# Attention output computed with tokens on partitions and added to x from its PSUM bank

## The reference

```python
x = x + 0.5 * ffn(layernorm(x))      # layer 0 of the kernel's expert code
x = x + attention(layernorm(x))      # Q = x@Wq+bq, 16 heads of 128, K and V of 4 groups; softmax(Q K^T / sqrt(128)) V, then @ Wo + bo
x = x + 0.5 * ffn(layernorm(x))      # layer 1
# ffn: 64 experts; the 8 largest router logits of each token choose its experts and weights;
# an expert takes its first 32 tokens (in the order of tokens), h = silu(x w1) * (x v1), y = h w2;
# the weighted y are added back to their tokens
```

## Time and profile before

| | |
|---|---|
| median of 3 runs | 665.5 us (663.27, 665.5, 667.88) |
| the profiled execution | 667.9 us, span 666.0 us |
| busy of the span | PE 94%, PE weight load 79%, VectorE 75%, ScalarE 59%, GpSimd 8% |
| the chain that ended last | PE 72%, VectorE 12%, ScalarE 6%, DMA 6%, issue 2% |
| granted PE clock, mean | 0.971 |

### The profile page before, as it was taken

One profiled execution on the slowest core, in us unless ns is written; L12 is line 12 of the kernel. 1 busy time (PEld: TensorE's weight loads), 2 busy tenths in 40 slices (PEclk: granted clock), 3 DMA queues, 4 the chain that ended last, 5 costly groups with the idle time before them and its releaser, 6 DMA issues.

```text
span 666.0 us, 11671 instructions
## 1 busy us (share of the span) xinstructions
PE 626.7 (94%) x4320; PEld 525.8 (79%) x4320; DVE 498.3 (75%) x1309; ACT 391.1 (59%) x1053; POOL 52.4 (8%) x75
## 2 busy tenths in 40 slices
PE   8589999999999999999999999999999999887995
PEld 6367677999888888888888888888888888665774
DVE  6746668889988677887777788876778877773663
ACT  5634475767666566566556666666666656662441
POOL 3443000000000000000000000000000000134210
PEclk9689999999999999999999999999999999969998
DMA  8999940000000000000000000000000034266991
GB/s 318 341 416 419 376 153 1 2 1 1 0 1 1 1 1 0 1 1 1 0 1 1 1 0 1 1 1 0 1 1 2 0 127 190 110 207 228 419 376 48
DMA packets 27619, 62.50 MB, mean 94 GB/s; under 512 B 7014, under 2 KB 17382, under 8 KB 27558
## 3 DMA queue, kind: packets, MB, share of 16 engines
q1 hardware_dynamic: 25398, 55.97, 22.2%
q0 software_dynamic: 1664, 5.30, 2.1%
q10 hardware_dynamic: 496, 0.43, 0.3%
HBM read 54.34 MB, written 7.34 MB: 93 GB/s over the span
## 4 chain that ended last, share of the span: by engine, by line
PE 72%; DVE 12%; ACT 6%; DMA 6%; issue 2%; POOL 1%; SPq 0%; POOLq 0%; DVEq 0%; ACTq 0%
PE bank L1406 18%; PE bank L1408 17%; PE bank L1407 17%; PE bank L1462 7%; PE bank L1217 3%; DMA slots<-token_table,slot_index 3%; DMA down_r<-down_in 3%; PE bank L1257 2%; ACT probs L728 2%; PE bank L1225 2%; PE bank L1267 2%; ACT probsT_hi L739 1%; DVE q_lo L1073 1%; ACT q_hi L711 1%; DVE probsT_lo L1129 1%
## 5 line engine op out<-in xcount | busy, mean ns | idle before, releaser
L728 ACT ACTIVATE probs<-bank,negmax 128x256 f32<-128x256 f32 x256 | 121.4, 494 | 1.8 <-DVE negmax L1087 1.6
L739 ACT CAST probsT_hi<-bank 128x512 fp32r<-128x512 f32 x128 | 68.8, 590 | 70.9 <-PE bank L1462 70.9
L711 ACT ACTIVATE o_hi<-bank,bv 128x512 fp32r<-128x512 f32 x64 | 44.1, 690 | 69.2 <-PE bank L1408 69.2
L1129 DVE TENSOR_TENSOR probsT_lo<-bank,probsT_hi 128x512 fp32r<-128x512 f32 x128 | 81.7, 679 | 0.4 <-ACT probsT_hi L739 0.4
L1087 DVE TENSOR_REDUCE negmax<-bank 128x2 f32<-128x512 f32 x128 | 81.7, 679 | 0.0
L1095 DVE TENSOR_SCALAR probs<-probs,rowinv 128x256 f32<-128x256 f32 x256 | 73.0, 348 | 2.3
L1073 DVE SCALAR_TENSOR_TENSOR o_lo<-bank,bv,o_hi 128x512 fp32r<-128x512 f32 x64 | 48.0, 749 | 34.5 <-ACT o_hi L711 34.5
L1408 PE MATMUL bank<-k_hi,q_lo 128*128 128x256 f32 x256 | 72.4, 283 | 0.0
L1407 PE MATMUL bank<-k_lo,q_hi 128*128 128x256 f32 x256 | 72.3, 283 | 0.0
L1406 PE MATMUL bank<-k_hi,q_hi 128*128 128x256 f32 x256 | 72.2, 282 | 0.0
L1073 DVE SCALAR_TENSOR_TENSOR q_lo<-bank,bq,q_hi 128x512 fp32r<-128x512 f32 x64 | 47.9, 748 | 32.2 <-ACT q_hi L711 31.9
(11 more groups left out here) (184 smaller groups left out, 1294.9 us busy)
## 6 DMA issues: line engine op xcount, KB each, us to landing
up_r<-up_in SPq DMA_DIRECT2D x16, 768.0 KB, 9.3
down_r<-down_in SPq DMA_DIRECT2D x14, 512.0 KB, 11.1
up_q<-up_in SPq DMA_DIRECT2D x8, 768.0 KB, 8.8
up_o<-up_in SPq DMA_DIRECT2D x6, 768.0 KB, 14.6
down_q<-down_in SPq DMA_DIRECT2D x8, 512.0 KB, 9.6
token_table<-xn SPq DMA_DIRECT2D x16, 256.0 KB, 2.4
down_o<-down_in SPq DMA_DIRECT2D x6, 512.0 KB, 16.3
x<-x_in SPq DMA_DIRECT2D x4, 512.0 KB, 5.5
```

Source lines behind the costliest of these rows:

```text
L711: nc.scalar.activation(dst, src, ACT.Identity, bias=bias).then_inc(work_high, 1)
L728: nc.scalar.activation(probs[:, n % 2, t, :], scores_ps[head][:, qt * S:qt * S + S], ACT.Exp, bias=negmax[:, n % 2, t:t + 1], accum_out=ro ...
L739: nc.scalar.copy(probsT[0][:, head].rearrange("p c s -> p (c s)"), probsT_ps[head][:]).then_inc(probsT_high, 1)
L1129: nc.vector.tensor_tensor(probsT[1][:, head].rearrange("p c s -> p (c s)"), probsT_ps[head][:], probsT[0][:, head].rearrange("p c s -> p ( ...
```

## The change

The operands of the output product are exchanged: `o` is stationary and `wo` moves (256 columns), so that `out_ps[bb]` holds 128 tokens on partitions, with the two tiles of a batch side by side. All products run one step late with 12 matmuls of 256 columns. `yT`, its copy, its transposes and the `work_ps` banks they used are gone; VectorE adds `out_ps[bb]` to x directly, batch 0 at step 15 and batch 1 at step 1 of the next block. The bias is added to x beforehand from `bo_row`, a row of `bo` on all partitions, which ScalarE and two PE matmuls of layer 0 make. At step 12 the product is split around the projections, and at step 16 it comes after the second projection. For the last block, the moments of tiles 0 to 11 move into steps 11 and 12. The low halves of some weights are made a little earlier. In layer 1 the wide `take_tokens` comes ahead of the codes, and `keep_busy(16)` behind the narrow part becomes 12. `wait_for_gathers` waits for four gathers where it waited for two, and in layer 0 SP waits until the last group's weights have landed before it issues the loads of wk, wq, wv and wo.

```diff
@@ -354,7 +334,8 @@
         first_fills = [("xT", 0, 0), ("xT", 1, 0), ("k", 0, 0), ("q", 0, 0), ("q", 1, 0), ("v", 0, 0),
                        ("q", 2, 0), ("q", 3, 0), ("v", 1, 0)]
         SCORES_AT = 6
-        SPREAD_AT = (5, 6, 7, 9)
+        SPREAD_AT = (5, 6, 7, 10)
+        BIAS_AT = ((13, 14), (4, 8))
...
             def wait_for_gathers(layer):
 
-                for n in range(2):
+                for n in range(IN_FLIGHT - 1):
...
             for g in range(4):
@@ -448,6 +429,7 @@
                 load(0, g)
             for g in range(AHEAD, GROUPS):
                 load_when_free(0, g)
+            sp.wait_ge(home(0, GROUPS - 1)[2], 16 * loads_before(0, GROUPS - 1))
...
                 copy_logits(3)
-                if layer == 1:
-                    act.wait_ge(y_ready, 2 * BLOCKS)
+                if layer == 0:
+                    act.wait_ge(small_loaded, 64)
+                    for kd in range(KD):
+                        nc.scalar.activation(bo_row[:, kd * P:kd * P + P], ident[:], ACT.Identity, scale=0.0,
+                                             bias=bo[:, kd:kd + 1]).then_inc(bo_spread, 1)
+                else:
+                    act.wait_ge(y_raw, 2 * BLOCKS)
                     make_code_ident()
                 act.wait_ge(moments_ready, layer + 1)
...
                 act.wait_ge(moments_ready, 2 * layer + 1)
                 normalise(first, TILES)
                 warm(ACT.Silu)
+                if layer == 0:
+                    act.wait_ge(bo_crossed, 1)
+                    nc.scalar.copy(bo_row[:], bank[5][:, D:2 * D]).then_inc(bo_ready, 1)
                 act.wait_ge(slotsT_raw, sT_seen.add())
                 nc.scalar.copy(slotsT[:, 0, :, :].rearrange("p k t -> p (k t)"), bank[0][:, 0:KD * P]).then_inc(slotsT_ready, 1)
...
                 jobs = fills(n, last)
-                if i > 0 and n in (2, 3):
-                    act.wait_ge(y_raw, y_seen.add())
-                    take_output(n - 2)
...
                 for job in jobs:
                     take_fill(*job)
-                if i > 0 and n in (2, 3):
-                    uses[0] += 1
-                take_high(o[0][:, home_of_o(n), :, :], bv[:, kv:kv + 1])
+                take_high(o[0][:, n % 2, :, :], bv[:, kv:kv + 1])
...
             copy_tokens(3)
-            act.wait_ge(y_raw, y_seen.add())
-            for d in range(KD):
-                take_output(d)
             expert_layer(1)
...
             late_moments = moment_steps(4, TILES)
-            in_fill = {1: 3, 2: 4, 3: 5, 4: 6, 6: 7, 7: 8, 8: 9}
+            in_fill = {1: [3], 2: [4], 3: [5], 4: [6, 7], 5: [8], 6: [9]}
...
-            def add_output(i, d):
-
-                dve.wait_ge(y_ready, y_seen.add())
-                xa = x[:, i * 4:i * 4 + 4, d * P:d * P + P]
-                nc.vector.tensor_tensor(xa, xa, work_ps[uses[0] % 2][:].rearrange("p (t c) -> p t c", t=4), ALU.add).then_inc(work_taken, 1)
-                uses[0] += 1
-                taken.add()
-
-            def last_output(i):
-
-                for pair in range(2):
-                    dve.wait_ge(y_ready, y_seen.add())
-                    xa = x[:, i * 4 + 2 * pair:i * 4 + 2 * pair + 2, :].rearrange("p t d -> p (t d)")
-                    last = nc.vector.tensor_tensor(xa, xa, work_ps[uses[0] % 2][:], ALU.add).then_inc(work_taken, 1)
-                    uses[0] += 1
-                    taken.add()
-                nc.vector.sem_inc(attention_done, 1)
-                dve.wait_ge(work_taken, taken.now())
-                nc.vector.memset(last_token[:, 0:1], 0.0)
-                for t in range(4):
-                    last = nc.vector.bn_stats(stats[:, i * 4 + t, :], x[:, i * 4 + t, :])
-                return last
+            def add_bias(i, bb):
+
+                xa = x[:, 4 * i + 2 * bb:4 * i + 2 * bb + 2, :]
+                nc.vector.tensor_tensor(xa, xa, bo_row[:].unsqueeze(1).to_broadcast([P, 2, D]), ALU.add).then_inc(bias_added, 1)
+
+            def add_output(i, bb):
+
+                dve.wait_ge(y_raw, y_seen.add())
+                dve.wait_ge(bias_added, 2 * i + bb + 1)
+                xa = x[:, 4 * i + 2 * bb:4 * i + 2 * bb + 2, :].rearrange("p t d -> p (t d)")
+                nc.vector.tensor_tensor(xa, xa, out_ps[bb][:], ALU.add).then_inc(out_added, 1)
+
+            def spread_of(i, t):
+
+                dve.wait_ge(out_added, 2 * i + t // 2 + 1)
+                return nc.vector.bn_stats(stats[:, 4 * i + t, :], x[:, 4 * i + t, :])
...
@@ -1141,14 +1113,21 @@
                     take_fill(*job)
                 if n == 9 and not last:
                     normalise_tokens(i + 1)
-                if added and n in (2, 3):
-                    add_output(i - 1, n - 2)
-                take_low(*[t[:, home_of_o(n), :, :] for t in o], bv[:, kv:kv + 1])
-                if added and n in SPREAD_AT:
-                    dve.wait_ge(work_taken, taken.now())
-                    a = 4 * (i - 1) + SPREAD_AT.index(n)
-                    nc.vector.bn_stats(stats[:, a, :], x[:, a, :])
-
+                if i is not None and n in BIAS_AT[i > 0]:
+                    add_bias(i, BIAS_AT[i > 0].index(n))
+                if i is not None and n == 15:
+                    add_output(i, 0)
+                if i is not None and i > 0 and n == 1:
+                    add_output(i - 1, 1)
+                take_low(*[t[:, n % 2, :, :] for t in o], bv[:, kv:kv + 1])
+                if i is not None and i > 0 and n in SPREAD_AT:
+                    spread_of(i - 1, SPREAD_AT.index(n))
+                if last and n in (11, 12):
+                    for moment in steps_of_last[6 * (n - 11):6 * (n - 11) + 6]:
+                        moment()
+
+            steps_of_last = moment_steps(0, TILES - 4)
+            dve.wait_ge(bo_ready, 1)
             dve.wait_ge(x_final, 4)
             normalise_tokens(0)
             for n, job in enumerate(first_fills):
@@ -1157,17 +1136,22 @@
                     maxima(0)
                 if n == SCORES_AT + 1:
                     normalise_probs(0)
-                if n in in_fill:
-                    split_low(in_fill[n])
+                for m in in_fill.get(n, []):
+                    split_low(m)
             step(0)
...
             for n in range(1, STEPS):
                 step(n, BLOCKS - 1, last=True)
-            masks(1, 0, moment_steps(0, TILES - 4))
             shifts(0, TILES - 4)
-            tie(last_output(BLOCKS - 1))
+            for t in range(2):
+                spread_of(BLOCKS - 1, t)
+            masks(1, 0)
+            add_output(BLOCKS - 1, 1)
+            nc.vector.sem_inc(attention_done, 1)
+            spread_of(BLOCKS - 1, 2)
+            tie(spread_of(BLOCKS - 1, 3))
             steps = moment_steps(TILES - 4, TILES)
             masks(1, 1, steps[:7])
             masks(1, 2, steps[7:])
...
                     pe.wait_ge(x_loaded[u // 2], 16)
                 elif u >= TILES // 2 - 2:
-                    pe.wait_ge(work_taken, issued.now(back=TILES // 2 - 1 - u))
+                    pe.wait_ge(out_added, 2 * (BLOCKS - 1) + u - (TILES // 2 - 2) + 1)
...
                 logits_of(layer, 3)
+                if layer == 1:
+                    take_tokens()
...
                 last.then_inc(codes_raw, 1)
-
-                take_tokens(layer)
-                if layer == 1:
-                    keep_busy(16)
+                if layer == 0:
+                    pe.wait_ge(bo_spread, KD)
+                    for kd in range(KD):
+                        last = mm(bank[5][:, D + kd * P:D + kd * P + P], bo_row[:, kd * P:kd * P + P], ident[:], start=True, stop=True)
+                    last.then_inc(bo_crossed, 1)
+
+                if layer == 0:
+                    take_tokens()
+                else:
+                    take_narrow_tokens()
+                    keep_busy(12)
                 pe.wait_ge(first_ready, keys_seen.add())
...
-            def output_product(n):
-
-
+            def output_product(n, i, halves=range(2)):
+
+
+                n %= STEPS
                 kv, bb, hp = place(n)
-                on_chip(("o", n % STEPS))
+                on_chip(("o", n))
                 split_by(O_SPLIT[kv])
-                for d in range(KD):
+                if i > 0 and n in (0, 2):
+                    pe.wait_ge(out_added, 2 * i - 1 + bb)
+                for qt in halves:
                     for head in range(2):
-                        last = three(out_ps[d][:, bb * S:bb * S + S], [a[:, G * kv + 2 * hp + head, d * P:d * P + P] for a in wo],
-                                     [a[:, home_of_o(n), head, :] for a in o], n % STEPS == 0 and head == 0,
-                                     n % STEPS == STEPS - 1 and head == 1, shared=True)
-                if n % STEPS == STEPS - 1:
+                        h = G * kv + 2 * hp + head
+                        last = three(out_ps[bb][:, qt * D:qt * D + D], [a[:, n % 2, head, qt * P:qt * P + P] for a in o],
```

(39 more changed lines are left out.)

72 lines of the change are left out of this document (20 added, 52 removed).

## The result

The changed kernel took 658.51 us (median of 8, 656.42 to 661.2) against 667.27 for the kernel before (median of 8). One of those eight, at 2100 us, counts in the median and not in the ratio. The ratio is 0.9886, 95% interval 0.9862 to 0.9909, about 7.6 us less; by the medians it is 8.8. Four more sets of runs, each on another chip, gave 0.9906, 0.9871, 0.9876 and 0.9837. I had forecast 14.7 us; the change brings a little over half of that.

The account below looks back on a forecast made before the run. The PE was taken as the bound, with 72% of the chain. Attention -5.1, all behind it -9.9 and layer 0 +0.3 make -14.7 us, from the 665.5 median 650.8, forecast as 651 us, range 644 to 659.

Parts of the forecast that it names:

- Gathers and loads of layer 1: Layer 1: fourth gather's 3.5 us wait goes, loads then end late; -9.9 us for all behind attention, bounds -7 and -11.5.
- Routing, the first gather: Layer 1 routing: keys start earlier, tokens and fillers delay less, the table's landing limits; first gather -6.7 us, bounds -6.0 and -6.9.
- the 2.1 us of the masks: Layer 1 routing: moments leave VectorE's work ahead of the second masks, so the keys start about 2.1 us earlier.
- the 4.6 us of tokens and fillers: Layer 1 routing: wide tokens move ahead of the codes, fillers drop to 24, so the slot keys come 4.6 us sooner.
- Attention: All attention steps: sum of gains from dropped transposes and waits against dearer products, -5.1 us.
- Steps 2 and 3: Attention, blocks 1 to 3: yT transposes and work-bank wait go, 1.07 us less per step, six times, -6.4 us.
- the products: Other attention steps with output products: twelve matmuls of 256 columns cost 0.09 us more, 38 times, +3.4 us.
- the waits: Attention steps 12 and 16: moved output products shrink PE waits, 0.35 us in seven places, -2.4 us, bounds 0 and -3.
- The last block: Attention's last block: steps 11 and 12 have one product less, VectorE gets moments; -1.0 us, bounds 0 and -2.7.
- rival (c): Attention blocks 1 to 3: output products wait for o_lo in every step, +22 us, time about 674; chance 0.05.
- Layer 0: Layer 0: last group's weights land sooner, attention's weight loads start later; +0.3 us, bounds -0.7 and +2.5.
- rival (b): Attention: waits of steps 2, 3, 12 and 16 come back elsewhere, attention +1 to +3, time 657 to 660; chance 0.12.

Follow-up runs that it names:

- sets 2 to 4: Three sets of follow-up runs, each on its own chip beside the kernel before; the unchanged changed kernel took 658.91, 657.0 and 659.06 us in them.
- wait_two: Changed kernel with layer 1's loads held behind two gathers instead of four: 659.67 us, ratio 0.9888 to the kernel before.
- wait_five: Changed kernel with layer 1's loads held behind all five gathers issued at once instead of four: 658.43 us, ratio 0.9859 to the kernel before.
- changed_fifth: Changed kernel run unchanged a fifth time, on another chip: 656.2 us, ratio 0.9837 to the kernel before.
- before_again: Kernel before, unchanged, run again beside the changed kernel's third run: 664.72 us in one execution.
- routing_alone: Kernel before plus only layer 1's routing part (wide tokens ahead of codes, twelve fillers, loads behind the fourth gather): 662.76 us against 666.08, ratio 0.993.
- early_exps: Changed kernel with layer 1's exponentials taken by ScalarE after eight normalised tiles instead of twelve: 655.2 us, one run.
- wide_late: Changed kernel with layer 1's wide tokens behind the codes again and sixteen fillers: 663.68 us, ratio 0.9959 to the kernel before.
- attention_alone: Changed kernel with wide tokens behind the codes, sixteen fillers, loads behind two gathers and no SyncE wait in layer 0: 661.22 us, ratio 0.9903.
- moments_in_four: Changed kernel with the last block's moments in portions of 4, 4 and 3 instead of 6 and 5: 656.22 us, one run.
- set 5: Fifth set of runs: the unchanged changed kernel, 656.2 us, and the same without layer 0's SyncE wait, 654.26 us.
- sets 1 and 5: Set 1 ran single-edit kernels without an unchanged changed kernel (kernel before 666.08 us); set 5 has its own line.

## Why the prediction was wrong

The direction held, and 658.5 lies in the range, but the effect was put at nearly twice its size. By the steps of the prediction:

**Gathers and loads of layer 1: this step failed.** Of the 9.9 us for all behind attention, 3.2 were for what comes after the first gather, and 1.4 were measured. I took the 3.51 us wait for the fourth gather and 1.3 us of slow steps behind it as won in full, as if nothing else held the PE in those steps. What the runs showed in its place is a late semaphore ahead of the second slot step. It came in every kernel of sets 2 to 4, the kernel before among them, and was 1.6 to 3.0 us late in four of the five profiles of the changed kernel; in three of these four the half clock followed. The fourth gather lands while the PE is held by it, so the wait that I removed isn't there to be won: wait_two and wait_five moved the time by nothing measurable. From the first gather to the end the changed kernel with the late semaphore takes 62.5 us in the mean, the kernel before 62.7. Where it doesn't come, the term holds as far as one profile of the kernel before can tell: 4.3 to 4.9 us in the first four slot steps for the 4.8 forecast, and 59.8 us to the end in changed_fifth for 64.0. I had read one execution, the slowest of three, as the kernel; a second one (before_again) shows the other case.

I had also set the wait against a rule of the Trainium skill ("DMA: Bandwidth & Descriptors", "Queues, rings and completion order": an engine alternates between the queue rows it has work for) and let the row win. By the DMA packets of the traces the first gathers land 2.5 to 3.5 us after their issue, and the fourth and fifth, in the kernels that wait for two and so have loads beside them, after 5.0 to 6.6 us. They are slowed, but they don't stand behind all the loads, which last about 39 us. So the trace agrees with the rule, and a gather slowed in this way still cost 3.51 us in the one profile where the PE was there first.

The loads I had nearly right: their last packet is through at 639.2 in the first profile of the changed kernel (forecast 640.6), though their first one comes 1.0 us after the issue and not 2. In the changed kernel the last group waits for them by 0.24 us at most. In routing_alone it waits 1.65 us, and the half clock follows from 647.5 to 650.9; of its 4.8 us from the gathers only 0.9 reached the end.

**Routing, the first gather: right in kind, 1.6 us too large.** 6.7 forecast, 5.1 measured in all five profiles. VectorE lost 2.1 us to GpSimd's multiply, for which the sum had no term. early_exps shows that with these back the table's stores hold the gather, 0.1 us of gain, and with the stores reordered 1.0. Of the two parts the 2.1 us of the masks came out (2.2 to 2.5 in wide_late, though attention_alone lost them again at the half clock), and the 4.6 us of tokens and fillers did not: 3.0 in routing_alone, 2.7 from wide_late to the changed kernel.

**Attention: -5.1 forecast, -4.1 measured.** Steps 2 and 3 gave 1.08 each, 6.5 in all, as forecast; the products cost 0.09 a step as the row said, not 0.015 as by the 2.5 ns of the Trainium skill ("TensorE: Matmul & The Clock Gate", "Wait — 56ns, not 53.3ns?"), in 28 places and not 38 (+2.6 for +3.4); block 0 +1.9 for +1.8. Of the waits only step 16 improved, 9.73 to 9.26, and step 12 got 0.13 to 0.19 worse, since half a product is too little cover for xT_lo: -0.9 for -2.4, though step 10 gave 0.7 that I hadn't counted. The last block gave +0.2 for -1.0: step 11 lost its 1.27, steps 12 and 13 took 1.47 back. moments_in_four shows that 0.6 of that is the moments; in the rest the PE waits for probsT_lo of VectorE, 1.19 and 0.94 us, with no projection to cover it. The splits at the start gave 0.8 for 0.5, and rival (c), products that wait for o_lo, never showed. (Its time should have been 673, not 674.)

**Layer 0: +0.3 forecast, +1.5 measured.** The landing of wo (94.6, forecast 93 to 94) was seen, the rest of the queue not: wk, wq and wv are late for ScalarE too. Of the 1.5 us about 0.6 is the wait: from the first xn transpose to step 0 it is 16.4 us without it and 17.0 or more with it. By the medians of set 5 the kernel without the wait is 1.9 us faster; the two profiles of that set don't show where that comes from. Why step 0 is some 1 us later than before even then stays open; the starts scatter by over 1 us between executions of one kernel (106.8 and 105.3 before).

**The measure.** The forecast started from an execution of 667.9 us and was subtracted from the median. Part of what it removed was what made that execution slow. That 658.5 falls where rival (b) put it says nothing for (b): attention got 4.1 us shorter, not longer.

## What to carry to other kernels

Take a second profile before a wait is priced: a wait that differs between two executions of the same kernel can be won only in the executions that have it, and one that lies beside another wait is worth only what it sticks out. When several chains meet, an edit of one is worth only the distance to the next: here 1.6 us of VectorE's chain brought 0.1 us until the table's stores were moved too. And a wait set ahead of a queue delays everything behind it: list all that the queue carries, not only the transfer it is meant for.

## What the runs showed of the hardware

**Late semaphores.** In 13 of the 20 profiles the semaphore of the PE's first up product of layer 1 came 0.8 to 3.0 us behind the product's end (0.04 us in the other seven), and ScalarE's gate started only then. They came in every kernel of three sets (2, 3 and 4) and in the first profile of the changed kernel, and in none of the kernels of sets 1 and 5; the same traces lack many semaphore events later on. In set 5 the changed kernel took 656.2 us, in the three sets with them 657.0 to 659.1; the kernel before took 665.7 to 667.5 in those three and 666.1 and 666.5 in sets 1 and 5, so it hardly differs. That fits: without the late semaphore it waits for the fourth gather instead, though only one such profile shows it. What causes them stays open; in wait_five the loads go out at 601.67, behind all five gathers and behind the product's end at 599.93, and it was still 1.9 us late, which rules out the loads that start beside the last gathers.

**VectorE and GpSimd.** A GpSimd multiply of 128x512 held a 128x32 conversion for 1.25 instead of 0.17 us, a 128x128 integer instruction for 1.30 instead of 0.29 and a 128x32 cast for 0.61 instead of 0.18, each until a multiply ended; MAX8 and MATCH_REPLACE8 ran beside it at full speed. The Trainium skill ("SBUF — State Buffer", "Who interferes with whom") says that VectorE shares one pair of its ports with GpSimd under an exclusive lock, that a cast or a tensor_scalar can take the pair for the whole instruction, and that an instruction with two inputs in SBUF contends with GpSimd's reads; the trace agrees.

**The clock.** In the first slot steps of layer 1 the PE's granted clock fell to the half level at other places from one execution of the same kernel to the next: 600.0 to 606.8, 602.9 to 606.3, not at all, 603.6 to 607.0 and not at all in the five profiles of the changed kernel. Where it fell the PE had waited just before (0.89 and 0.57 us for gathers in the first profile), but the third profile has such waits (0.92 and 0.82 us) and no fall. From the third up product to the fourth it is 3.0 us at the full level (changed_fifth) and 4.0 us with the half level in it (the first profile).
